# Pooled attention scores from 32-row tiles of TensorE instead of stacked operands

## The chip, the cores and the metric

The kernel runs on one core of one Trainium2 chip. The metric is the device time of one execution in microseconds. A core has TensorE (PE, matmuls, with its weight loads shown apart as PEld), VectorE (DVE), ScalarE (ACT), GpSimd (POOL), and SyncE (SP), which issues DMAs here.

## The reference

The input x is (4, 256, 32, 32): 4 images of 256 channels and 1024 pixels. Two residual blocks follow one another.

```python
x = x + L0(groupnorm(x))     # windowed attention (4 heads) beside pooled attention (4 heads)
x = x + L1(groupnorm(x))     # mask from the image's centre of mass, relu, 3x3 convolution
# pooled attention, per image: 1024 queries, 256 keys (means of 2x2 pixels), heads of 32
q = (xh.reshape(B, H*W, C) @ l_q_w).reshape(B, H*W, 4, 32)
k, v = (pooled @ l_kv_w) ...
attn = softmax(einsum('bnhd,bmhd->bhnm', q, k) * 32**-0.5)
lo = einsum('bhnm,bmhd->bnhd', attn, v)
# L1: mu = rounded centres of mass of x over rows and columns, per channel
mask = max(1 - (|posX - mu_x| + |posY - mu_y|) * mask_weight, -1)
out = conv3x3(relu(x * mask)) + bias
```

## The kernel before

The four images are taken one after the other. An image b passes `front(b)` (projections, pooled scores for their maxima, window scores) and `rest(b)` (softmax weights, sums, output projections, residual). The second block of image b-1 (statistics, mask, convolution) is laid between the steps of image b: its convolution is a list of 144 matmuls that TensorE works off in helpings, `conv.more(n)`, whose sizes stand in the tables FRONT and REST (lines 67 to 70). Image 0 has no convolution beside it, and neither has `front(1)`; there, `keep_warm` matmuls (table WARM) fill some gaps. Every engine has a written-out program, and semaphores order them against each other. What stands in an engine's program behind a wait stands still with it.

Precise products. Operands are split into a high part rounded to fp32r and a low remainder; a product is hi*hi + hi*lo + lo*hi, three matmuls for the projections. For the pooled scores the heads have 32 rows each, so the three products are made in one matmul of 96 rows: SyncE stacks the parts in SBUF, `qs` holding hi, lo, hi and `ks` hi, hi, lo of each head on rows 0 to 95 (`stack`, lines 240 to 254, six DMAs per image). `lq_hi`, `lq_lo`, `lk_hi`, `lk_lo` are made by ACT and DVE (lines 398, 400, 622, 627) from `slot[0]` and `slot[1]`. For this the columns of the pooled query and key weights are mixed on the host, so that the four heads of one dimension lie on neighbouring rows.

Largest scores. The softmax needs the maximum of each query over its 256 keys. TensorE computes the scores of 8 blocks of 128 queries (lines 969 to 992), 4 heads x 256 keys per block, into three PSUM slots of two banks each (LA_SLOT), and DVE reduces each block (`maxima`, line 633). The negated maxima are transposed (line 999), split in two (lines 641, 643), and SyncE lays them on rows 96 and 97 of `qs` (`stack_maxima`), against two rows of ones in `ks`. The scores proper, transposed (keys on partitions), are then 8 tiles of two matmuls of 98 rows and 512 columns (`pooled_scores`, line 904), each followed by an exponential on ACT (`exp_scores`, line 434). Tiles 0 and 1 stand in `front`, 2 and 3 and then 4 to 7 in `rest`. Their PSUM slots alternate (ST_SLOT). When all eight are exponentiated, `by_head` (line 912) sums them on column tiles of 32 columns.

Order around the change. On DVE, `front(b)` runs: the low parts; `masks(b-1)`, the statistics of the older image (17 to 20 small operations at its end, L505 to L517); `mask_parts(b-1)`, a chain of 16 small operations (L561 to L583); the maxima of blocks 0 to 5, 6 and 7; their split; `masked_image(b-1)` (L590), which waits for POOL's `mask_sum` (L297); the tiles of the convolution and the window softmax. POOL forms the products of queries and keys (L305), for which it waits until `mask_parts(b-1)` is through, and then the mask sums; in image 0 it prepares the convolution's weights around them (L313 to L341). ACT's program in `front(b)`: copies of the projections, the normalised older image (L415), `rectify` (L421) of its first half, then the copy of the window scores (L447), which TensorE transposes (L1008) for the window softmax.

TensorE's first block of largest scores waits for all six stacks (line 971), its later ones for the maxima of earlier blocks.

Of the kernel before, what the change touches and what calls it, by code (L numbers as in the profile page):

```python
# [5 lines left out]
F32 = mybir.dt.float32  # L6
# [6 lines left out]
P = 128  # L13
B, C, H, W = 4, 256, 32, 32
KT = C // P
# [10 lines left out]
SC = 3 * HD  # L26
SM = SC + 2
# [22 lines left out]
WCOLS = 6 * P  # L50


LA_SLOT = (0, 1, 2, 0, 1, 2, 0, 1)
ST_SLOT = (0, 1, 0, 1, 1, 0, 2, 1)
# [44 lines left out]
def build(nc, x, wqkv, whp, wlp, bh, bl, cw, cb, mw, filt, consts, selectors, out):  # L99
    with ExitStack() as ctx:  # L100
# [24 lines left out]
        qs = sb("qs", [P, HEADS, HW], F32R)  # L125
        ks = sb("ks", [P, HEADS, G], F32R)
# [10 lines left out]
        lq_hi, lq_lo = probs[:, 0].bitcast(F32R), probs[:, 1]  # L137
        lk_hi, lk_lo = probs[:, 2, 0:G].bitcast(F32R), probs[:, 2, G:2 * G]
# [50 lines left out]
        stacked, max_stacked = sem("stacked"), sem("max_stacked")  # L189
# [19 lines left out]
        def img(b, k, lo=0, n=HW):  # L209

            at = (b % RING) * KT * HW + k * HW + lo
            return xy[:, at:at + n]

# [7 lines left out]
        def _(sp):  # L221
# [18 lines left out]
            def stack(b):  # L240

                def rows(to, part, parts):
                    sp.dma_start(to[HD * part:HD * (part + 1)].bitcast(F32), parts.bitcast(F32)).then_inc(stacked, 16)  # L243

                sp.wait_ge(lq_act, b + 1)
                rows(qs, 0, lq_hi)
                rows(qs, 2, lq_hi)
                sp.wait_ge(lq_dve, b + 1)
                rows(qs, 1, lq_lo)
                sp.wait_ge(lk_act, b * 2 + 1)  # L250
                rows(ks, 0, lk_hi)
                rows(ks, 1, lk_hi)
                sp.wait_ge(lk_dve, b + 1)
                rows(ks, 2, lk_lo)

            def stack_maxima(b):

                sp.wait_ge(lm_dve, (b + 1) * 2)
                for i, t in enumerate((lm_hi, lm_lo)):
                    sp.dma_start(qs[SC + i:SC + i + 1].bitcast(F32), t.bitcast(F32)).then_inc(max_stacked, 16)  # L260

            def step(b, first, last):
# [3 lines left out]
                if not last:  # L266
                    stack(b + 1)
# [9 lines left out]
            stack(0)  # L277
# [9 lines left out]
        STACK, MAX_STACK = 6 * 16, 2 * 16  # L287
# [3 lines left out]
        def _(pool):  # L291
# [65 lines left out]
            nc.gpsimd.tensor_tensor(w_lo[:], raw_w, w_hi[:].bitcast(F32), ALU.subtract).then_inc(w_split, 1)  # L357
            pool.wait_ge(w_split, 2)
# [7 lines left out]
        def _(act):  # L366
# [28 lines left out]
            def projections(b, first):  # L395
                wait_count(act, lpv_pe, b)
                act.wait_ge(proj_pe, b * 5 + 1)
                nc.scalar.copy(lq_hi, flat[0]).then_inc(lq_act, 1)
                act.wait_ge(proj_pe, b * 5 + 2)
                nc.scalar.copy(lk_hi, slot[1][:, 0, 0:G]).then_inc(lk_act, 1)  # L400
# [743 lines left out]
```

## Time and profile before

| | |
|---|---|
| median of 3 runs | 425.68 us (424.81 to 427.03) |
| the profiled execution | 424.92 us, its span 423.1 us |
| TensorE matmuls busy | 336.3 us, 79% of the span, 1544 instructions |
| TensorE weight loads | 237.4 us, 56% |
| VectorE | 293.3 us, 69% |
| ScalarE | 114.1 us, 27% |
| GpSimd | 100.5 us, 24% |
| mean granted TensorE clock | 0.883 of full speed |

Times in rows are microseconds from the start of the span, means are ns. A matmul's duration contains its way through the array, so consecutive ones overlap: their pace is read from the starts, or from a merged row's length over its count. "<-" behind a group in brackets names what ended the idle time before it, and how long that was.

### The profile page before, as it was taken

The page shows a single profiled execution, that of the slowest core. Times are in us where ns is not written, and L with a number is a line of the kernel's source. Part 1 is how long each engine was busy: PE and PEld are TensorE (multiplying, and loading weights), DVE is VectorE, ACT ScalarE, POOL GpSimd, SP SyncE. Part 2 cuts the span into 40 slices and gives each one's busy share as a digit, 9 for nine tenths or more (in the row PEclk, how much of TensorE's full clock was granted, in tenths as well). Part 3 has the DMA queues.
Part 4 walks back from the last instruction along what each step waited for, and adds up shares of the span by engine and source line. Part 5 has one row for each costly group of instructions (what it writes and reads, how often), then busy time and mean ns, then how long its engine had stood idle before and what let it go on. Part 6 is the DMA issues. An engine that isn't in the chain of part 4 may idle for free.

```text
span 423.1 us, 4092 instructions
## 1 busy us (share of the span) xinstructions
PE 336.3 (79%) x1544; PEld 237.4 (56%) x1544; DVE 293.3 (69%) x584; ACT 114.1 (27%) x124; POOL 100.5 (24%) x58
## 2 busy tenths in 40 slices
PE   2580967899498599991999599965999999806996
PEld 1360725347374474681868373854877648705885
DVE  4940739877976987887679776896678658885121
ACT  2230014522402536133026243122046300231000
POOL 0288499200083020000910200006600200030000
PEclk9896895799859599997799989995999999965999
DMA  7579300006900000079000400293001001001011
GB/s 243 210 95 155 136 4 0 2 0 84 102 2 3 1 2 1 2 132 104 0 5 0 149 2 0 79 117 42 2 3 50 2 0 52 0 0 50 2 50 50
DMA packets 8611, 20.38 MB, mean 48 GB/s; under 512 B 1680, under 2 KB 4624, under 8 KB 8336
## 3 DMA queue, kind: packets, MB, share of 16 engines
q1 hardware_dynamic: 8592, 20.13, 23.8%
q8 instruction: 12, 0.20, 0.2%
q14 instruction: 7, 0.06, 0.1%
HBM read 7.93 MB, written 4.19 MB: 29 GB/s over the span
## 4 chain that ended last, share of the span: by engine, by line
PE 41%; issue 19%; DVE 16%; DMA 12%; POOL 5%; ACT 3%; SPq 2%; POOLq 0%; DVEq 0%; ACTq 0%
PE slot L838 18%; PE cps L870 17%; DMA ks<-probs 10%; PE cps L838 4%; POOL probs L305 4%; DMA xy<-x 2%; SPq L243 2%; DVE st L488 2%; ACT probs L434 1%; DVE gn L516 1%; POOL mask L297 1%; DVE v_lo L615 1%; PE slot L1008 1%; PE slot L1031 1%; DMA out<-xy 1%
## 5 line engine op out<-in xcount | busy, mean ns | idle before, releaser
L870 PE MATMUL cps<-v_hi,cw_hi 128*128 128x496 f32 (+1 forms) x192 | 79.1, 412 | 19.5 <-DVE xy L670 15.1
L870 PE MATMUL cps<-v_hi,cw_lo 128*128 128x496 f32 (+1 forms) x192 | 78.7, 410 | 0.0
L870 PE MATMUL cps<-v_lo,cw_hi 128*128 128x496 f32 (+1 forms) x192 | 77.8, 405 | 0.0
L305 POOL TENSOR_TENSOR probs<-q_w,k_w 128x1024 f32<-128x1024 f32 x16 | 37.3, 2363 | 139.2 <-DVE rw L583 132.2
L633 DVE TENSOR_REDUCE l_max<-slot 128x4 f32<-128x1024 f32 x32 | 37.7, 1220 | 33.5 <-PE slot L838 33.5
L870 PEld LDWEIGHTS cps<-v_hi,cw_hi 128*128 128x128 f32 x192 | 38.4, 200 | 32.9 <-ACT v_hi L428 20.6
L838 PE MATMUL slot<-ks,qs 96*128 96x256 f32 x128 | 26.5, 362 | 35.6 <-DMA ks<-probs 34.8
L838 PEld LDWEIGHTS slot<-ks,qs 96*128 96x128 f32 x128 | 23.8, 257 | 39.6 <-DMA ks<-probs 36.6
L870 PEld LDWEIGHTS cps<-v_hi,cw_lo 128*128 128x128 f32 x192 | 38.1, 198 | 8.4 <-issue 0.7
L870 PEld LDWEIGHTS cps<-v_lo,cw_hi 128*128 128x128 f32 x192 | 38.2, 199 | 7.1
L434 ACT ACTIVATE probs<-slot 128x1024 f32<-128x1024 f32 x32 | 31.7, 1024 | 36.1 <-PE slot L838 36.0
L838 PE MATMUL slot<-xn_hi,w_hi 128*128 128x512 f32 x60 | 25.1, 419 | 4.5 <-DVE xn_lo L526 4.5
L353 POOL TENSOR_TENSOR q_w<-q_w,k_w 128x1024 f32<-128x1024 f32 x4 | 9.6, 2391 | 75.8 <-DVE k_w L755 75.8
L421 ACT ACTIVATE xn<-mask 128x1024 f32<-128x1024 f32 x8 | 8.5, 1059 | 63.2 <-DVE mask L590 63.1
L838 PE MATMUL slot<-qs,ks 98*128 98x512 f32 x64 | 22.9, 468 | 2.0 <-DMA qs<-probs 1.7
L838 PE MATMUL slot<-xn_hi,w_lo 128*128 128x512 f32 x60 | 24.5, 408 | 0.0
L838 PE MATMUL slot<-xn_lo,w_hi 128*128 128x512 f32 x60 | 24.3, 405 | 0.0
L297 POOL TENSOR_TENSOR mask<-rw 128x1024 f32<-128x1024 f32 x8 | 15.2, 1916 | 38.2 <-DVE rw L583 38.2
L488 DVE BATCH_NORM_STATS2 st<-xy 128x6 f32<-128x512 f32 x32 | 19.8, 679 | 4.5 <-DMA xy<-x 4.5
L668 DVE SCALAR_TENSOR_TENSOR xy<-cps,cbias,xy 128x512 f32<-128x512 f32 x16 | 12.0, 748 | 14.8 <-PE cps L870 14.6
L838 PE MATMUL slot<-probs,cst 128*32 128x512 f32 x176 | 20.4, 596 | 1.9 <-ACT probs L434 1.9
L428 ACT CAST v_hi<-mask 128x1024 fp32r<-128x1024 f32 x16 | 16.7, 1046 | 14.2 <-DVE mask L608 7.2
(143 smaller groups left out, 545.4 us busy)
## 6 DMA issues: line engine op xcount, KB each, us to landing
qs<-probs SPq DMA_DIRECT2D x12, 512.0 KB, 10.6
xy<-x SPq DMA_DIRECT2D x8, 512.0 KB, 9.2
out<-xy SPq DMA_DIRECT2D x8, 512.0 KB, 2.6
raw_cw<-conv_w SPq DMA_DIRECT2D x2, 1152.0 KB, 7.5
ks<-probs SPq DMA_DIRECT2D x12, 128.0 KB, 13.6
probs<-h_qkv SPq DMA_DIRECT2D x2, 192.0 KB, 4.6
probs<-l_kv SPq DMA_DIRECT2D x2, 128.0 KB, 4.0
probs<-selectors SPq DMA_DIRECT2D x1, 256.0 KB, 4.0
```

What stands on the lines that cost most here:

```text
L243: sp.dma_start(to[HD * part:HD * (part + 1)].bitcast(F32), parts.bitcast(F32)).then_inc(stacked, 16)
L297: nc.gpsimd.tensor_tensor(mask[:, k].rearrange("p (h w) -> p h w", h=H), rw[:, k, 0].unsqueeze(2).to_broadcast([P, H, W]), rw[:, k, 1].uns ...
L305: nc.gpsimd.tensor_tensor(qk[:, j].rearrange("p (n w) -> p n w", n=NW), q_w[:].rearrange("p (n w) -> p n w", n=NW), k_w[:, j * G:(j + 1) * ...
L353: nc.gpsimd.tensor_tensor(pv[0], pv[0], pv[1], ALU.add).then_inc(pv_pool, 1)
L421: nc.scalar.activation(xn[:, k], mask[:, k], ACT.Relu).then_inc(relu, 1)
L428: nc.scalar.copy(v_hi[:, k, 2 * phase:2 * phase + 2].rearrange("p a b -> p (a b)"), mask[:, k]).then_inc(v_act, 1)
L434: nc.scalar.activation(probs[:, i], flat[ST_SLOT[i]], ACT.Exp, scale=SCALE / NW)\
L488: last = nc.vector.bn_stats(s[:, k, half], img(self.b, k, half * HALF, HALF))
L633: nc.vector.tensor_reduce(l_max[:, bass.ds(n, HEADS, step=NB)], flat[LA_SLOT[n]].rearrange("p (h m) -> p h m", h=HEADS), AX_X, ALU.max, ne ...
L668: ins = nc.vector.scalar_tensor_tensor(y, cps[:, pos], cbias[:, o:o + 1], y, ALU.add, ALU.add)
L838: return nc.tensor.matmul(dst, lhsT, rhs, start=start, stop=stop)
L870: ins = nc.tensor.matmul(cps[:, pos % 2, y0 * WT:y1 * WT], (cw_hi, cw_hi, cw_lo)[part][:, k, pos, dy + 1, o * P:(o + 1) * P], (v_hi, v_lo, ...
```

## The change

The stacks by DMA and the tiles `qs` and `ks` go. The columns of the pooled query and key weights are put in the order of the heads when they are split at the start (six parts each on ACT and POOL in place of one), so that head h lies on rows 32h to 32h+31 of `lq_hi`, `lq_lo`, `lk_hi`, `lk_lo`, which get tiles of their own. Each product of the split is a matmul of its own on the 32 rows of its head, and the products accumulate in PSUM, in a bank per head: step by step, the four heads of a step behind one another. The maxima go to rows 32h and 32h+1 of a tile `top`, against a tile of ones, as a fourth step of two rows. Largest scores are made for two blocks at a time (24 matmuls of 256 columns), and the scores proper in four parts (16 matmuls of 512 columns), each followed by two exponentials. On DVE, the mask chain `mask_parts(b-1)` moves behind the maxima and their split. POOL's products wait for the statistics of the older image instead of its mask chain.

```diff
-            def stack(b):
-                def rows(to, part, parts):
-                    sp.dma_start(to[HD * part:HD * (part + 1)].bitcast(F32), parts.bitcast(F32)).then_inc(stacked, 16)
...
             def stack_maxima(b):
...
-                    sp.dma_start(qs[SC + i:SC + i + 1].bitcast(F32), t.bitcast(F32)).then_inc(max_stacked, 16)
+                    sp.dma_start(top[i:P:HD].bitcast(F32), t.bitcast(F32)).then_inc(max_stacked, 16)
...
-            stack(0)
             load(1)
             load(2)
...
-                wait_count(pool, mask_c, b * N_MASK)
+                wait_count(pool, gn_c[1], b * N_GN)
                 products(b)
...
-            nc.gpsimd.tensor_tensor(w_lo[:], raw_w, w_hi[:].bitcast(F32), ALU.subtract).then_inc(w_split, 1)
+            for (lo, hi), source in zip(weight_parts(w_lo, w_hi), weight_sources()):
+                nc.gpsimd.tensor_tensor(lo, source, hi.bitcast(F32), ALU.subtract).then_inc(w_split, 1)
...
+                    part, pair = divmod(i, 2)
+                    t, half = divmod(part, 2)
                     act.wait_ge(st_pe, b * LT + i + 1)
-                    nc.scalar.activation(probs[:, i], flat[ST_SLOT[i]], ACT.Exp, scale=SCALE / NW)
+                    nc.scalar.activation(probs[:, pair * 2 * MT + t:pair * 2 * MT + t + MT + 1:MT,
+                                               half * HALF:(half + 1) * HALF],
+                                         slot[ST_SLOT[part][pair]][:], ACT.Exp, scale=SCALE / NW)
...
                 if not first:
                     masks(b - 1)
-                    mask_parts(b - 1)
                 maxima(b, range(6))
                 older_result(V_SUM)
                 maxima(b, range(6, NB))
                 maxima_parts(b)
+                if not first:
+                    mask_parts(b - 1)
                 older_result(V_DIFF)
...
+            def pooled_scores(b, part):
+                t, half = divmod(part, 2)
+                m, q = slice(t * P, (t + 1) * P), halves(half)
+                for step in range(4):
+                    for h in range(HEADS):
+                        r = rows_of(h)
+                        to = slot[ST_SLOT[part][h // 2]][:, h % 2]
+                        if step < 3:
+                            ins = mm(to, (lk_hi, lk_hi, lk_lo)[step][r, m], (lq_hi, lq_lo, lq_hi)[step][r, q],
+                                     step == 0, False)
+                        else:
+                            r = slice(HD * h, HD * h + 2)
+                            ins = mm(to, one[r], top[r, q], False, True)
+                            if h % 2:
+                                ins.then_inc(st_pe, 1)
+
+            def largest_scores(b, n):
+                for block in range(2):
+                    q = slice((n + block) * P, (n + block + 1) * P)
+                    for step in range(3):
+                        for h in range(HEADS):
+                            r = rows_of(h)
+                            ins = mm(slot[LA_SLOT[n + h // 2]][:, h % 2, block * G:(block + 1) * G],
+                                     (lq_hi, lq_lo, lq_hi)[step][r, q], (lk_hi, lk_hi, lk_lo)[step][r],
+                                     step == 0, step == 2)
+                            if step == 2 and block == 1 and h % 2:
+                                ins.then_inc(la_pe, 1)
...
-                for n in range(NB):
+                for n in range(0, NB, 2):
                     if n == 0:
-                        pe.wait_ge(stacked, (b + 1) * STACK)
-                        pe.wait_ge(qkv_sb, b * 3 + 2)
...
+                    else:
+                        pe.wait_ge(la_max, b * NB + n - 1)
+                        if n == 2 and not first:
                             pe.wait_ge(gn_c[1], (b - 1) * N_GN + GN_SENT + 1)
...
+                    largest_scores(b, n)
...
                     conv.more(FRONT[2 + n])
+                    conv.more(FRONT[3 + n])
                     if starting:
                         keep_warm(WARM[1 + n])
...
-                for i in range(2, LT - NW):
-                    pe.wait_ge(st_exp, b * LT + i - 1)
-                    pooled_scores(b, i)
-                    conv.more(REST[1])
+                pe.wait_ge(st_exp, b * LT + 2)
+                pooled_scores(b, 1)
+                conv.more(2 * REST[1])
...
-                for i in range(LT - NW, LT):
-                    if i < LT - 1:
-                        pe.wait_ge(pv_ready, b * NW + i - 2)
-                    else:
-                        pe.wait_ge(st_exp, b * LT + 5)
-                    pooled_scores(b, i)
-                    conv.more(REST[4])
+                for part in range(2, NW):
+                    pe.wait_ge(pv_ready, b * NW + part + 1)
+                    pe.wait_ge(st_exp, b * LT + part + 2)
+                    pooled_scores(b, part)
+                    conv.more(2 * REST[4])
```

The helper `weight_parts` yields the query, key and value columns, the pooled value columns, and for each of the two channel tiles the pooled query and the pooled key columns; `weight_sources` yields the same from the raw weights, with the mixed columns put in order. `maxima` reads the two heads and two blocks of a slot and writes them to their places in `l_max`.

## Rows read from the trace of the kernel before

**Rows 1.** Waits: engine, line, releaser: us in total, times, longest.
```profile
PE slot L838 <- DMA ks<-probs: 34.8, 4, 10.9
```
**Rows 2.** DMA issues: count, KB of each, median us from issue to landing.
```profile
ks<-probs SPq DMA_DIRECT2D x12, 128.0 KB, 13.6
```
**Rows 3.** Busy time by stretch: the stalls of images 0, 2 and 3, and after.
```profile
core 0: us, PE busy (x) PEld busy (x) DVE busy (x) ACT busy (x) POOL busy (x), PEclk, DMA share, GB/s
30.50:41.40 10.90, 0.01 (x1) 0.00 (x0) 0.00 (x0) 1.01 (x1) 9.88 (x7) 0.70 1.06 130
...
192.40:201.30 8.90, 0.00 (x0) 0.00 (x0) 6.43 (x35) 3.38 (x3) 1.20 (x1) 0.66 0.89 98
...
281.90:290.80 8.90, 0.18 (x1) 0.00 (x0) 6.63 (x35) 3.38 (x3) 0.99 (x1) 0.62 0.90 99
290.80:296.90 6.10, 6.07 (x20) 5.37 (x21) 3.49 (x3) 0.00 (x0) 6.10 (x4) 0.50 0.00 1
```
**Rows 4.** Timeline of PE and its loads: start, length, engine, operation, count.
```profile
47.38 1.60 PE L838 MATMUL slot<-ks,qs 96*128 96x256 f32 x12
...
163.08 3.64 PE L838 MATMUL slot<-probs,cst 128*32 128x512 f32 x32 [0.21 <-ACT probs L434]
165.25 0.13 PEld L838 LDWEIGHTS slot<-probs,cst 128*32 128x32 f32 x4 [0.30 <-issue]
166.65 1.98 PE L838 MATMUL slot<-q_w,w_out 128*128 128x512 f32 x4
...
183.03 0.30 PEld L838 LDWEIGHTS slot<-w_hi,p_w 128*128 128x128 f32 x2
```
**Rows 5.** Timeline of the start and of image 0's front.
```profile
10.13 3.45 POOL L357 TENSOR_TENSOR w_lo<-probs,w_hi 128x1536 fp32r<-128x1536 f32 x1 [9.19 <-ACT w_hi L440]
10.32 3.27 DVE L516 SCALAR_TENSOR_TENSOR gn<-gn 128x2 f32<-128x2 f32 x1
...
30.55 1.01 ACT L407 COPY k_w<-slot 128x1024 f32<-128x1024 f32 x1 [1.79 <-PE slot L838]
...
37.07 3.56 POOL L326 TENSOR_TENSOR cw_lo<-raw_cw,cw_hi 128x768 fp32r<-128x768 f32 x2
...
47.62 9.30 POOL L305 TENSOR_TENSOR probs<-q_w,k_w 128x1024 f32<-128x1024 f32 x4 [6.99 <-PE cps L838]
```
**Rows 6.** Timeline of the rest of image 0.
```profile
64.03 1.94 ACT L434 ACTIVATE probs<-slot 128x1024 f32<-128x1024 f32 x2 [1.97 <-PE slot L838]
...
67.77 1.97 PE L1031 MATMUL slot<-cst,k_w 128*128 128x128 f32 x8 [0.53 <-DVE k_w L657]
...
74.78 2.36 DVE L755 TENSOR_TENSOR xn<-slot,v_w 128x1024 f32<-128x1024 f32 x2 [0.18 <-PE slot L838]
...
80.58 2.78 PE L838 MATMUL slot<-probs,cst 128*32 128x512 f32 x24 [1.30 <-ACT probs L434]
```
**Rows 7.** Timelines of DVE, ACT and PE in image 3's front.
```profile
285.75 0.16 DVE L517 SCALAR_TENSOR_TENSOR gn<-gn 128x2 f32<-128x2 f32 x1
...
304.37 1.23 DVE L633 TENSOR_REDUCE l_max<-slot 128x4 f32<-128x1024 f32 x1 [0.23 <-PE slot L838]
...
309.60 1.00 ACT L447 COPY q_w<-slot 128x1024 f32<-128x1024 f32 x1
...
311.52 1.04 PE L1008 MATMUL slot<-cst,q_w 128*128 128x128 f32 x8
```
**Rows 8.** Timeline of DVE in the tail: mask chain's end, first masked image.
```profile
369.57 0.19 DVE L583 TENSOR_SCALAR rw<-rw 128x64 f32<-128x64 f32 x1
...
371.79 2.91 DVE L590 SCALAR_TENSOR_TENSOR mask<-mask,xn 128x1024 f32<-128x1024 f32 x1 [2.02 <-POOL mask L297]
```
**Rows 9.** Timeline of DVE: end of statistics and start of softmax, image 2.
```profile
196.05 0.16 DVE L517 SCALAR_TENSOR_TENSOR gn<-gn 128x2 f32<-128x2 f32 x1
...
221.90 0.29 DVE L650 TENSOR_REDUCE s_max<-slot 128x32 f32<-128x128 f32 x1 [1.57 <-PE slot L1008]
```
**Rows 10.** Timelines of DVE and PE: last maxima and transposes of image 1.
```profile
129.16 2.36 DVE L633 TENSOR_REDUCE l_max<-slot 128x4 f32<-128x1024 f32 x2 [4.56 <-PE slot L838]
...
135.72 1.09 PE L1008 MATMUL slot<-cst,q_w 128*128 128x128 f32 x8 [1.94 <-ACT q_w L447]
```

More of the change, by code:

```diff
@@ L25 @@
 LT = HEADS * MT
-SC = 3 * HD
-SM = SC + 2
 NB = HW // P
@@ L124, in build @@
         v_w = sb("v_w", [P, HW])
-        qs = sb("qs", [P, HEADS, HW], F32R)
-        ks = sb("ks", [P, HEADS, G], F32R)
+        lq_hi, lq_lo = sb("lq_hi", [P, HW], F32R), sb("lq_lo", [P, HW], F32R)
+        lk_hi, lk_lo = sb("lk_hi", [P, G], F32R), sb("lk_lo", [P, G], F32R)
+        top = sb("top", [P, HW], F32R)
+        one = sb("one", [P, P], F32R)
         lv = sb("lv", [P, MT, P])
@@ L212, in img, with weight_parts, weight_sources @@
             return xy[:, at:at + n]
+        def weight_parts(*tiles):
+            yield [t[:, :, 0:WLQ] for t in tiles]
+            yield [t[:, :, WLV:WCOLS] for t in tiles]
+            for k in range(KT):
+                for c0 in (WLQ, WLK):
+                    yield [t[:, k, c0:c0 + P].rearrange("p (h d) -> p h d", h=HEADS) for t in tiles]
+        def weight_sources():
+            yield raw_w[:, :, 0:WLQ]
+            yield raw_w[:, :, WLV:WCOLS]
+            for k in range(KT):
+                for c0 in (WLQ, WLK):
+                    yield raw_w[:, k, c0:c0 + P].rearrange("p (d h) -> p h d", h=HEADS)
         def run(step):
@@ L439, in step @@
                     act.wait_ge(w_in, 3 * KT * 16)
-                    nc.scalar.copy(w_hi[:], raw_w).then_inc(w_split, 1)
+                    for (hi,), source in zip(weight_parts(w_hi), weight_sources()):
+                        last_part = nc.scalar.copy(hi, source)
+                    last_part.then_inc(w_split, 1)
                     normalise_first()
@@ L810, in _ @@
             nc.vector.tensor_copy(sel[:].rearrange("p a b -> p (a b)"), raw_sel).then_inc(w_ready, 1)
-            nc.vector.memset(ks[SC:SM].bitcast(F32), 1.0).then_inc(ones, 1)
+            nc.vector.memset(one[:].bitcast(F32), 1.0).then_inc(ones, 1)
             nc.vector.scalar_tensor_tensor(mwf[:, 2], mwf[:, 1], 1.0, mwf[:, 0], ALU.is_equal,
@@ L902, in project, with rows_of @@
                 last.then_inc(proj_pe, 1)
-            def pooled_scores(b, i):
-                h, t = divmod(i, MT)
-                for half in range(2):
-                    last = mm(slot[ST_SLOT[i]][:, half], ks[0:SM, h, t * P:(t + 1) * P], qs[0:SM, h, halves(half)],
-                              True, True)
-                last.then_inc(st_pe, 1)
+            def rows_of(h):
+                return slice(HD * h, HD * (h + 1))
+            def pooled_scores(b, part):
[24 more added lines that the diff above has]
+                                ins.then_inc(la_pe, 1)
             def by_head(s, lhsT, ready):
@@ L978, in front @@
                             pe.wait_ge(qkv_sb, b * 3 + 3)
-                    elif n == 2:
-                        if not first:
+                    else:
+                        pe.wait_ge(la_max, b * NB + n - 1)
+                        if n == 2 and not first:
                             pe.wait_ge(gn_c[1], (b - 1) * N_GN + GN_SENT + 1)
-                    else:
-                        pe.wait_ge(la_max, b * NB + n - 2)
-                    for h in range(HEADS):
-                        ins = mm(flat[LA_SLOT[n]][:, h * G:(h + 1) * G], qs[0:SC, h, n * P:(n + 1) * P], ks[0:SC, h],
-                                 True, True)
-                    ins.then_inc(la_pe, 1)
+                    largest_scores(b, n)
                     if first and n == 2:
@@ L1014, in front @@
                 pe.wait_ge(max_stacked, (b + 1) * MAX_STACK)
-                for i in range(2):
-                    pooled_scores(b, i)
+                pooled_scores(b, 0)
                 conv.more(FRONT[12])
```

48 lines of the change are left out of this document (18 added, 30 removed).

## The prediction

> **What bounds the kernel now.** I read the waits first: TensorE (PE) loses 34.8 us in four waits for the stacked key rows, the largest item it has [rows 1]. The stack DMAs take 13.6 us (median) from issue to landing [rows 2]. Taken alone that promises 35 us. So I read, for each wait, what the other engines did in it, in the busy times by stretch [rows 3]. In image 0 VectorE (DVE) stands still (0.00 of 10.9 us), but GpSimd (POOL) is busy 9.88 us with the convolution weights. In images 2 and 3 (image 1 repeats it) DVE is busy 6.43 and 6.63 of 8.9 us: it does the statistics and the mask chain of the older image, behind which the maxima queue. The granted clock is 0.62 to 0.70 over these stretches, that is, it falls from 2.4 to 1.2 GHz in each, and 0.50 in the 6.1 us of dense work after the last one. Most of the stall is therefore covered, and the question is what comes last once it is gone.
>
> **How fast row tiles run.** No row tile of 32 rows stands in this trace. The nearest rows are the column tiles of by_head: 32 instructions of 512 columns take 3.64 us while the same type at full width takes 1.98 us for 4 [rows 4]. That is 0.43 us for one full-width instruction and 0.43 us for four column tiles: four run at once, and four loads sit in 0.13 us. Full-width fp32r at 256 columns goes at 1.60/12 = 0.13 us, 0.117 us without the tail of the last; I double this at half clock [rows 4]. A pair of blocks is now 24 matmuls in place of 8. Four at once: 6 x 0.117 = 0.7 us, plus 0.2 to 0.3 us for two changes between tile shapes (3.64 us for eight groups of 0.43 leaves 0.2) = 1.0 us against 0.94 before. One at a time: 24 x 0.117 = 2.8 us. I take four at once. A scores part is 16 matmuls of 512 columns for what were 4: 0.93 us four at once (3.7 us one at a time), so only the shape changes are added.
> TensorEngine Tiling (Array Packing), in the Trainium skill, says under "Key Properties" that tiles work independently but that a change of tiling mode drains TensorE; under "PSUM Pressure" it says different row tiles may not share a bank, which the change respects. TensorE: Matmul & The Clock Gate (Trainium skill), Part 3, states 3.07x measured for four row tiles of 512 columns; by it a part would take 3.7/3.07 = 1.2 us, an estimate 0.3 us over mine, or 1.2 us an image.
>
> **Start: -0.9 us (0 to -1.8).** One w_lo subtraction of 3.45 us becomes six. From the subtractions of 768 and 1536 columns (about 1.8 and 3.45 us [rows 5]) POOL's fixed part is 0.2 us, so six take 4.5 us; ScalarE's (ACT) six casts take about 2.2 us for 1.47. w_lo ends at 15.3 us, before PE needs it (17.4). But now a DVE operation of normally 0.16 us stands for 3.27 us, exactly to the end of POOL's [rows 5]: they exclude each other. Shorter and later pieces let the chain through earlier by 0.8 to 1.6 us. The loads of images 1 and 2, which SP now issues after the convolution weights with no stack in front, queue behind these weights; I cost them at nothing.
>
> **Image 0, front: -7.0 us (-4.4 to -7.5).** k_w is copied by 31.56 [rows 5], so the pairs start there, not at 41.46. The V projection then ends by 37. What is last now is POOL: its convolution weights end at 40.63, and only then do the products start (47.62 now). The gain is 7.0, not 10. The products and the window scores follow at the old pace. If the clock falls in the 2.3 us before the first product, the last scores and the transposes cost 2.6 more.
>
> **Image 0, rest: +3.7 us (+2.7 to +4.7).** Each part fills both slots and releases its two exponentials at its end; the next part waits for them. Before, tiles alternated between the slots. Part 0 ends at 64.85 as now, its exps run 64.9 to 66.8 (now 64.0 to 66.0), part 1 runs 66.9 to 68.9 and pushes the transposes from 67.77: +1.2 [rows 6]. Part 2 needs the third product (76.0, now 77.2): 1.9 us at half clock, one exp 1.0, part 3 1.9, two exps 2.0, joints 0.3: by_head at 84.3 where it was 80.58.
>
> **Images 1 to 3, front.** The maxima can begin when the statistics end, S, ahead of the 16 operations of the mask chain, 3.7 us earlier than now. Image 3: S is 285.9 [rows 7]; the first pair runs at 283.1 to 284.0 (v_w copied); maximum 0 ends at 287.1; pair 1.0, 13 convolution matmuls 3.0, pair 1.0, 10 of them 2.3, pair 1.0, two maxima 2.4: the maxima end at 297.8 where they ended at 305.6 [rows 7]. 7.8 us gained there. Now the bill. The transpose and the two splits take 1.2 us, the moved mask chain 3.8 us (16 small operations, none hidden). Then POOL's mask sum, which ran beside the maxima, is exposed. The tail of the kernel shows this very sequence: from the end of the chain at 369.77 to the end of the first masked image at 374.70 are 4.9 us, because the DVE operation (2.91 us in place of 1.21) also stands until POOL's second sum ends [rows 8]. SBUF — State Buffer, "Who interferes with whom", in the Trainium skill, states this: a VectorE instruction with two SBUF inputs and a GpSimd one that reads SBUF exclude each other; the trace agrees. Behind it ACT's queue holds rectify (as long) and then the copy of the window scores (1.00) [rows 7], for which PE waits. 297.8 + 1.2 + 3.8 + 4.9 + 2.0 = 309.7: the transposes come 1.8 us earlier than at 311.52, and PE has idled 5.9 us for it. By the stalls seen, its clock falls there: transposes 0.9 us longer (1.97 against 1.04 [rows 6, 7]), 1.5 us on what follows: +0.6. With weight 0.6 it has also fallen in the 3.1 us between the first pair and the second, which costs 2.0 more: **image 3 +1.9 us (-1.7 to +3.8)**.
> Image 2 likewise: S at 196.2, the maxima end at 208.1, the transposes start at 220.1 against 221.0 (0.9 ahead of the softmax's first operation) [rows 9], clock +1.0, and 0.6 x 2.0, less where DVE and not PE is last: **+0.8 (-1.9 to +2.5)**. In image 1 there is no convolution yet to fill PE, and the warming matmuls between blocks 5 and 7 fall away: at half clock a pair takes 1.6 us, the maxima end at 124.8 (131.5 now), the transposes start at 136.8 (135.7 now) [rows 10] and take 0.9 longer: **+1.9 (-0.6 to +2.8)**.
>
> **Images 1 to 3, rest: +1.5 us (0 to +3.6).** Four parts with 0.2 us of shape changes each, and one more exp behind the last part, under 8 convolution matmuls (1.8 us): 0.5 an image. The third product is there when part 2 wants it.
>
> **Sum:** -0.9 - 7.0 + 3.7 + 1.9 + 0.8 + 1.9 + 1.5 = +1.9. On the profiled execution's 424.9 that gives 426.8 us, no change that can be told from none (about 0.5%, 2.1 us, is what a measurement of this kernel can tell). The median shown, 425.7, lies 0.8 above the profiled execution, which the range takes in.
>
> **Rivals.**
> (a) Row tiles take turns: slower. Its place is the 96 + 64 matmuls per image, its point the pace: slower as soon as a pair takes clearly over 1.2 us. If only the loads (two of 128 columns in 0.30 us, of which one lasts 0.19: one per 0.11 us [rows 4]) take turns, a pair is 2.7 and a part 1.8 us: about 2 us on each of three pairs and 0.9 on each part, at half clock double: +10, +9, +8, +9 us on top, 463. If matmuls too: 2.8 and 3.7 us, some 485. For it: no row tile is in the trace. Against: column tiles plainly run four at once. Chance 0.12.
> (b) PE keeps its clock in the shorter gaps: faster. Image 0's rest is then +2.7, images 1 to 3 -0.6, -0.9, -1.2 and the rest 1.2: -7 us, 418. For it: the gaps of 3 us are half the old ones. Against: 5.9 us of new idling per image. Chance 0.20.
> (c) The stall was the bound and most of 34.8 us comes off: 390 to 400. DVE's and POOL's busy shares in it [rows 3] speak against. Chance 0.04.
> The forecast has 0.62, with its own range 421 to 432; 0.02 is left for what I don't see.
>
> **Chances and range.** Faster by over 0.5% is under 423.5: (b), (c) and a sixth of the forecast's own, 0.33. Slower by over 0.5% is over 427.8: (a) and 0.4 of the forecast's own, 0.39. The same: 0.28. The range reaches over (b), 415 to 434, and leaves out (a) and (c).
>
> **What would show it.** The pace of the 32-row matmuls (0.7 us for 24 of 256 columns); POOL's first products at 40 us; by_head of image 0 later relative to the products by 3.7; in images 1 to 3 maxima that end 7 us earlier and then a PE wait of 4 to 6 us for ACT's copy of the window scores; the masked image at 2.9 us instead of 1.2. The forecast is wrong if row tiles are slower than 0.12 us per group of four, if the clock stays up, or if DVE is not held by POOL's sum.

## The result and the profile after

| | kernel before | changed kernel |
|---|---|---|
| median of its runs, us | 425.6 (424.8 to 427.0) | 434.95 (433.8 to 436.4) |
| ratio to before | 1 | 1.022, 95% interval 1.017 to 1.027 |
| profiled execution, us | 424.9 | 433.85 |
| its span, us | 423.1 | 432.1 |
| mean granted clock | 0.883 | 0.869 |

The change costs 2.2%. The forecast was 426.8 with a range that ends at 434.0, so it had the direction and a fifth of the size.

The waits of the changed kernel (engine, line, what released it: us in total, times, longest) no longer have the 34.8 us of [rows 1]. New ones stand in their place:

```profile
POOL mask L294 <- DVE rw L586: 64.9, 4, 39.1
...
PE slot L1035 <- ACT q_w L450: 19.9, 4, 7.7
...
PE slot L845 <- DVE l_max L637: 14.1, 7, 2.9
...
DVE mask L593 <- POOL mask L294: 6.8, 4, 2.0
```

19.9 us of TensorE's new idle time stand ahead of the transposes of the window scores. The timeline of image 2 (start, length, engine, line, operation) shows the sequence behind that wait on VectorE, GpSimd, ScalarE and TensorE:

```profile
210.83 0.28 DVE L647 CAST probs<-slot 32x128 fp32r<-32x128 f32 x1 [0.42 <-PE slot L1026]
...
214.95 0.20 DVE L586 TENSOR_SCALAR rw<-rw 128x64 f32<-128x64 f32 x1
...
215.23 3.78 POOL L294 TENSOR_TENSOR mask<-rw 128x1024 f32<-128x1024 f32 x2 [9.91 <-DVE rw L586]
...
217.18 4.05 DVE L593 SCALAR_TENSOR_TENSOR mask<-mask,xn 128x1024 f32<-128x1024 f32 x2 [1.37 <-POOL mask L294]
...
220.12 1.06 ACT L419 ACTIVATE xn<-mask 128x1024 f32<-128x1024 f32 x1 [21.95 <-DVE mask L593]
221.09 0.99 ACT L450 COPY q_w<-slot 128x1024 f32<-128x1024 f32 x1
...
222.14 1.97 PE L1035 MATMUL slot<-cst,q_w 128*128 128x128 f32 x8 [5.64 <-ACT q_w L450]
```

The maxima end at 210.4 (214.9 before), and then every step is exposed: 3.8 us of mask chain, GpSimd's sum, the masked image (4.05 us for two, of which the first takes 2.91 as in [rows 8]), rectify, copy. TensorE, which was busy up to its transposes before, stands idle for 5.64 us. Its clock falls: from the transposes at 222.14 it runs at 1.2 GHz for 7.9 us, to 230.0. A second slow stretch stands further back, from 247.7 to 254.0, behind a wait for the statistics of the next image. The busy times by stretch give the size of both together: from the transposes to by_head of image 2, before and after (columns as in [rows 3]):

```profile
220.80:252.80 32.00, 26.65 (x121) 21.22 (x119) 25.25 (x56) 13.16 (x15) 2.35 (x1) 0.95 0.14 50
```
```profile
222.10:259.70 37.60, 33.15 (x168) 24.30 (x170) 26.31 (x57) 14.00 (x16) 2.35 (x1) 0.80 0.11 42
```

32.0 us became 37.6, TensorE's busy time grew by 6.5 us, and its granted clock went from 0.95 to 0.80.

Where the 9.0 us of span came from, read from the start times of the same steps in both timelines (S is the end of the statistics of the older image, as in the prediction; us):

| stage | before | after | difference | forecast |
|---|---|---|---|---|
| start and image 0 up to its transposes | 59.98 | 52.19 | -7.8 | -7.9 |
| image 0, on to by_head | 20.60 | 23.44 | +2.8 | +3.7 |
| by_head of image 0 to S of image 1 | 33.51 | 35.64 | +2.1 | 0 |
| image 1, S to transposes, to by_head | 21.63, 27.36 | 23.04, 28.32 | +2.4 | +2.4 |
| image 2, S to transposes, to by_head | 24.61, 31.94 | 26.37, 37.52 | +7.3 | +1.3 |
| image 3, S to transposes, to by_head | 25.61, 25.00 | 25.70, 28.12 | +3.2 | +2.4 |
| by_head of images 1 and 2 to the next S | 33.14 | 33.14 | 0.0 | 0 |
| by_head of image 3 to the end | 86.6 | 85.5 | -1.1 | 0 |

The sum is +9.0 where +1.9 was forecast, and 6.0 of the 7.1 us of miss are in image 2. The lines of image 0's by_head and of the end scatter by more than a microsecond between kernels whose code there is the same (below), so little is built on them. The row tiles themselves ran as forecast. One part of the pooled scores in image 2 is four groups of four, 0.23 us apart:

```profile
236.03 0.51 PE L845 MATMUL slot<-lq_hi,lk_hi 32*128 32x512 f32 x4
236.37 0.41 PE L845 MATMUL slot<-lq_lo,lk_hi 32*128 32x512 f32 x4
236.60 0.41 PE L845 MATMUL slot<-lq_hi,lk_lo 32*128 32x512 f32 x4
236.83 0.41 PE L845 MATMUL slot<-top,one 2*128 2x512 f32 x4
237.17 0.49 PE L877 MATMUL cps<-v_hi,cw_hi 128*128 128x496 f32 x1
```

From 236.03 to 237.17 are 1.14 us, and a pair of blocks takes 0.91 us, read in the same way (299.99 to 300.90). In image 0 GpSimd's products start at 39.89 in place of 47.62 [rows 5], right behind its convolution weights, and the w_lo pieces hold VectorE for 1.66 us in place of 3.27:

```profile
11.30 1.66 DVE L520 SCALAR_TENSOR_TENSOR gn<-gn 128x2 f32<-128x2 f32 x1
...
36.29 3.63 POOL L323 TENSOR_TENSOR cw_lo<-raw_cw,cw_hi 128x768 fp32r<-128x768 f32 x2
39.89 9.24 POOL L302 TENSOR_TENSOR probs<-q_w,k_w 128x1024 f32<-128x1024 f32 x4
```

### The profile page after: what moved, and what is told of

Same layout as the page of the kernel before. It is cut to its first block, busy times and chain, and to the rows that moved or that the text cites. A ratio compares the mean times of both kernels' runs of the same rounds, so it can differ in the third digit from the quotient of the medians.

```text
span 432.1 us, 4949 instructions
## 1 busy us (share of the span) xinstructions
PE 343.4 (79%) x1976; PEld 230.4 (53%) x1976; DVE 298.1 (69%) x584; ACT 114.3 (26%) x129; POOL 103.1 (24%) x63
## 4 chain that ended last, share of the span: by engine, by line
PE 45%; DVE 21%; issue 19%; POOL 9%; ACT 3%; DMA 1%; POOLq 0%; SPq 0%; DVEq 0%; ACTq 0%
PE cps L877 22%; PE slot L845 20%; DVE st L491 2%; POOL probs L302 2%; DVE l_max L637 2%; POOL mask L294 2%; POOL cw_lo L323 2%; PE cps L845 2%; DVE mask L593 2%; ACT probs L434 1%; DVE xn L552 1%; DMA xy<-x 1%; PE slot L1035 1%; DVE q_w L762 1%; DVE xn L549 1%
## 5 line engine op out<-in xcount | busy, mean ns | idle before, releaser
L877 PE MATMUL cps<-v_hi,cw_hi 128*128 128x496 f32 (+1 forms) x192 | 80.1, 417 | 18.8 <-DVE xy L676 15.1
L877 PE MATMUL cps<-v_hi,cw_lo 128*128 128x496 f32 (+1 forms) x192 | 79.6, 415 | 0.0
L877 PE MATMUL cps<-v_lo,cw_hi 128*128 128x496 f32 (+1 forms) x192 | 78.9, 411 | 0.0
L877 PEld LDWEIGHTS cps<-v_hi,cw_hi 128*128 128x128 f32 x192 | 38.6, 201 | 33.5 <-ACT v_hi L426 19.8
L637 DVE TENSOR_REDUCE l_max<-slot 128x4 f32<-128x1024 f32 x32 | 37.6, 1219 | 18.6 <-PE slot L845 18.6
L845 PE MATMUL slot<-xn_hi,w_hi 128*128 128x512 f32 x60 | 25.2, 421 | 3.8 <-POOL w_lo L355 3.8
L845 PE MATMUL slot<-lk_hi,lq_hi 32*128 32x256 f32 x128 | 12.5, 380 | 18.5 <-DVE l_max L637 14.1
L845 PE MATMUL slot<-probs,cst 128*32 128x512 f32 x176 | 24.2, 692 | 2.1 <-ACT probs L434 2.0
L1035 PE MATMUL slot<-cst,q_w 128*128 128x128 f32 x32 | 7.0, 391 | 19.9 <-ACT q_w L450 19.9
L674 DVE SCALAR_TENSOR_TENSOR xy<-cps,cbias,xy 128x512 f32<-128x512 f32 x16 | 11.9, 747 | 13.4 <-PE cps L877 13.4
L593 DVE SCALAR_TENSOR_TENSOR mask<-mask,xn 128x1024 f32<-128x1024 f32 x8 | 16.2, 2061 | 6.8 <-POOL mask L294 6.8
L676 DVE SCALAR_TENSOR_TENSOR xy<-cps,xy 128x512 f32<-128x512 f32 x16 | 10.7, 687 | 14.4 <-PE cps L877 14.4
```

The costliest lines, as they stand in the source:

```text
L593: nc.vector.scalar_tensor_tensor(mask[:, k], mask[:, k], -1.0, xn[:, k], ALU.max, ALU.mult).then_inc(masked, 1)
L637: nc.vector.tensor_reduce(l_max[:, 0:HEADS * NB].rearrange("p (h n) -> p h n", n=NB) [:, 2 * pair:2 * pair + 2, block:block + 2], slot[LA_ ...
L674: ins = nc.vector.scalar_tensor_tensor(y, cps[:, pos], cbias[:, o:o + 1], y, ALU.add, ALU.add)
L676: ins = nc.vector.scalar_tensor_tensor(y, cps[:, pos - 2], (1.0, -1.0)[pos - 2], y, ALU.mult, ALU.add)
L845: return nc.tensor.matmul(dst, lhsT, rhs, start=start, stop=stop)
L877: ins = nc.tensor.matmul(cps[:, pos % 2, y0 * WT:y1 * WT], (cw_hi, cw_hi, cw_lo)[part][:, k, pos, dy + 1, o * P:(o + 1) * P], (v_hi, v_lo, ...
```

## The experiments

Theory A: the loss comes from the second half of the change, the mask chain behind the maxima. It puts chain, GpSimd's sum, masked image and rectify ahead of ScalarE's copy, and TensorE's idle time and the clock behind it are the price. Theory B: the row tiles cost it (changes of shape, both exponentials of a part at its end). All ratios are to the kernel before, run on the same chip in the same session; its median there was 425.6 to 427.1 us, so medians of different sessions compare to a microsecond or two.

| kernel | median us | ratio, 95% interval |
|---|---|---|
| changed kernel | 434.95 | 1.022, 1.017 to 1.027 |
| e1_chain_ahead | 422.8 | 0.992, 0.989 to 0.995 |
| e2_chain_behind | 450.9 | 1.057, 1.052 to 1.063 |
| e3_copy_first | 427.5 | 1.002, 0.998 to 1.005 |
| e4_warm | 436.9 | 1.025, 1.020 to 1.031 |
| e5_warm_fit | 428.0 | 1.008, 1.004 to 1.012 |
| e6_refill | 414.4 | 0.976, 0.969 to 0.982 |
| e7_ahead_copy | 422.7 | 0.992, 0.988 to 0.996 |
| e8_pool_free | 447.9 | 1.053, 1.046 to 1.059 |
| e9_refill_copy | 410.6 | 0.964, 0.959 to 0.969 |
| e10_before_refill | 422.6 | 0.992, 0.988 to 0.995 |
| e11_refill_warm0 | 414.1 | 0.973, 0.967 to 0.979 |
| e12_all | 410.35 | 0.964, 0.959 to 0.969 |

The same stages as above, in the profiled executions (us; for each of images 1, 2, 3: S to transposes, then transposes to by_head):

| kernel | S to transposes | transposes to by_head |
|---|---|---|
| before | 21.6, 24.6, 25.6 | 27.4, 31.9, 25.0 |
| changed | 23.0, 26.4, 25.7 | 28.3, 37.5, 28.1 |
| e1 | 20.2, 24.2, 23.1 | 28.3, 33.9, 26.3 |
| e2 | 27.8, 30.6, 30.5 | 28.5, 35.3, 26.1 |
| e3 | 16.4, 19.4, 20.8 | 33.9, 39.9, 33.5 |
| e4 | 25.0, 28.5, 28.5 | 28.4, 33.7, 26.2 |
| e5 | 23.0, 26.6, 26.5 | 27.9, 32.6, 26.4 |
| e6 | 20.1, 20.2, 20.9 | 28.1, 33.7, 25.9 |
| e9 | 16.5, 19.3, 19.3 | 31.0, 33.0, 26.0 |
| e10 | 20.4, 23.5, 22.0 | 27.2, 31.8, 25.0 |

### The two halves of the change, one by one

e1_chain_ahead is the changed kernel with the mask chain back in its old place:

```diff
-                wait_count(pool, gn_c[1], b * N_GN)
+                wait_count(pool, mask_c, b * N_MASK)
...
                 if not first:
                     masks(b - 1)
+                    mask_parts(b - 1)
                 maxima(b, range(6))
...
                 maxima_parts(b)
-                if not first:
-                    mask_parts(b - 1)
```

> The changed kernel with one part undone: the mask chain stands ahead of the maxima again and GpSimd's products wait for it again; row tiles, accumulation in PSUM and the missing stack DMAs stay. Theory A (the loss of the change lies in TensorE's idle time ahead of the window-score transposes, 19.9 us in four waits, 5.6 us each in images 2 and 3, and in the half clock behind it): GpSimd's mask sum hides beside the maxima again, the masked image takes 1.2 us in place of 2.9, ScalarE's copy comes some 3.5 us earlier in each of three images, and the clock stays up behind the transposes of image 2, worth 3 more: about 421 us, 418 to 425. Theory B (the row tiles themselves cost it, by changes of shape and by parts whose exponentials both come at the end): the time stays at 433 to 436.

e2_chain_behind makes the opposite edit in the kernel before: mask_parts behind maxima_parts, GpSimd's wait on gn_c[1]; the stacks stay.

> The kernel before with only the other part of the change: the mask chain behind the maxima, GpSimd's products let go by the statistics; stacks by DMA and full-width score matmuls stay. Theory A: before, the chain (3.8 us) ran inside the wait for the stacks, so moving it gives back nothing and exposes chain, GpSimd's sum, the slow masked image and rectify: 6 to 8 us in each of three images, 443 to 450 us. Theory B: the placement is worth little either way, 424 to 429 us.

Measured: 422.8 us, inside theory A's 418 to 425, and 450.9 us, just above its 443 to 450. Theory B falls as the account of the loss. Row tiles alone make the kernel 0.8% faster; the placement alone makes it 5.7% slower. But row tiles are not free: by the table e1 gains 4.4 us from S to the transposes of images 1 to 3 and gives 4.3 us back from the transposes to by_head (1.0, 2.0 and 1.3 us), so that its 0.8% comes from image 0. How much of the 4.3 us is the clock and how much the scores themselves is not taken apart here. In e1 GpSimd's sum (206.65 to 210.4) is done before the masked image asks for it, and the two masked images take 2.35 us and not 4.05 (timeline of VectorE, image 2):

```profile
212.80 0.76 DVE L674 SCALAR_TENSOR_TENSOR xy<-cps,cbias,xy 128x512 f32<-128x512 f32 x1
213.47 2.35 DVE L593 SCALAR_TENSOR_TENSOR mask<-mask,xn 128x1024 f32<-128x1024 f32 x2
```

In e2 the waits show both idle times of TensorE side by side, because the stacks still set the start of the maxima and moving the chain away gives nothing back:

```profile
PE slot L839 <- DMA ks<-probs: 35.1, 4, 11.1
PE slot L1009 <- ACT q_w L447: 21.6, 4, 9.5
```

By the table e2 loses 5 to 6 us from S to the transposes in each image, and up to 3.4 behind them. Beside row tiles the placement costs 12 us (434.95 against 422.8), not 24, since the maxima there do begin 3.7 us earlier. That gain stands in the prediction's sum; it is smaller than the bill. That the 12 us between 24 and 12 are this gain (3 x 3.7 = 11 us) is worked out, not measured by itself.

### The wait or the clock behind it

e3_copy_first takes the wait away by order alone:

```diff
                 if not first:
                     normalise_y(b - 1, b + 1)
-                    rectify(b - 1, 0)
                 act.wait_ge(ssum_pe, b + 1)
                 nc.scalar.copy(q_w[:], flat_cps if first else flat[0]).then_inc(ssum_sb, 1)
                 if not first:
+                    rectify(b - 1, 0)
                     rectify(b - 1, 1)
```

> The changed kernel, but ScalarE copies the window scores before it rectifies the first half of the masked image, so that the mask chain is no longer ahead of TensorE's transposes. Theory A: TensorE's wait for this copy goes from 19.9 us to under 4, the transposes come 6 us earlier, the clock stays up behind them; VectorE's softmax still stands behind the masked image, so of the 6 us only 1.5 and the clock's share (some 4 in image 2, 1 to 2 in images 1 and 3) come off: 425 to 429 us. Theory B: 433 to 436 us.

Measured: 427.5 us, inside theory A's 425 to 429. The wait did not vanish, it moved (waits of TensorE in e3): TensorE now comes early to the convolution of the new image and waits there for VectorE.

```profile
PE cps L877 <- DVE v_lo L618: 17.3, 3, 8.7
...
PE slot L1035 <- ACT q_w L449: 2.0, 2, 1.2
```

e4_warm and e5_warm_fit leave the order alone and put matmuls without a use into the wait (14 in e4; in e5 9 in image 1 and 7 in images 2 and 3, as shown):

```diff
                 conv.more(FRONT[11])
+                if not first:
+                    for _ in range(9 if starting else 7):
+                        mm(slot[1][:, 0, 0:C_ALL], cst[:, C_ID:C_ID + P], cst[:, 0:C_ALL], True, True)
                 pe.wait_ge(ssum_sb, b + 1)
```

> The changed kernel with 14 matmuls of 384 columns without a use (about 0.34 us each at 2.4 GHz, 4.8 us) into a free bank, ahead of the wait for ScalarE's copy of the window scores in images 1 to 3. The wait itself stays, only the clock behind it can change. If the half clock behind the wait is the larger part of the price: by_head of image 2 comes 4 us earlier, of image 3 and 1 about 2 us each, 427 to 430 us. If the wait itself is the price and the clock hardly matters: 434 to 436 us.

> As e4_warm, but the matmuls without a use are sized to end inside the wait: in e4_warm one took 0.66 us and not 0.34, so that the 14 took 9.2 us and pushed the transposes by 2 to 3 us an image, while from the transposes to by_head images 2 and 3 took 3.9 and 1.9 us less. Now 7 in images 2 and 3 (4.6 us in a wait of 5.6) and 9 in image 1. If the half clock is the price: the transposes come no later than in the changed kernel, by_head follows them 3.9 and 1.9 us sooner, 0.9 comes off the transposes of image 1: 427.5 to 430 us. If the shorter stage of e4_warm was only a catching up of what was lost before it: 434 to 436 us.

e4 gave 436.9 us, which taken alone would speak against the clock. Its trace says otherwise. I had the price of such a matmul wrong: it is two instructions and 0.66 us, so the 14 took about 9 us and pushed the transposes by 2.0, 2.1 and 2.8 us in images 1 to 3. In e5 they fit (timeline of TensorE, image 2):

```profile
216.91 4.68 PE L845 MATMUL slot<-cst 128*128 128x384 f32 x14
222.69 1.09 PE L1038 MATMUL slot<-cst,q_w 128*128 128x128 f32 x8 [1.11 <-ACT q_w L450]
```

The transposes come as late as ever (26.6 us behind S, 26.4 in the changed kernel), but they take 1.09 us and not 1.97, and the stretch behind them is (columns as in [rows 3])

```profile
222.70:255.30 32.60, 28.17 (x164) 20.85 (x164) 25.91 (x57) 13.91 (x16) 2.35 (x1) 0.95 0.13 49
```

32.6 us at a clock of 0.95 instead of 37.6 at 0.80. The same stretch is 0.45 us shorter in image 1 and 1.7 us in image 3, 7.1 us in all; 1.1 us are lost ahead of the transposes of images 2 and 3, so 6.0 are left, and the medians differ by 7.0 (434.95 and 428.0). The two profiled executions differ by only 4.0 us (433.85 and 429.87): 0.8 us in image 0 and 1.1 us behind by_head of image 3, where both kernels issue the same code, go the other way. e4 repeats the reading: from the transposes to by_head its images 2 and 3 take 3.9 and 1.9 us less than in the changed kernel. A kernel that does the changed kernel's work, with ScalarE's copy no earlier, gets back 6 to 7 of the 9 us when TensorE is kept busy until it comes. So of the loss against the kernel before the larger part is the clock behind the wait, not the wait. e1, which has neither in images 2 and 3, is 5 us faster than e5.

### VectorE beside GpSimd's products

e8_pool_free is e1 without the second edit: GpSimd's products are let go by the statistics and run beside the mask chain.

```diff
-                wait_count(pool, mask_c, b * N_MASK)
+                wait_count(pool, gn_c[1], b * N_GN)
```

> e1_chain_ahead, but GpSimd's products are let go by the statistics, as in the changed kernel, and so run beside the 16 operations of the mask chain. If VectorE's operations with two inputs and GpSimd's products exclude each other (in the changed kernel the masked image took 2.91 us in place of 1.21 beside GpSimd's sum), the first of them stands for up to 2.4 us, and those behind it for a product each where GpSimd is let in again: the chain takes 6 to 10 us in place of 3.7 and the time goes to 430 us or more. If they share, the chain stays at 3.7 us, the products end 3.7 us earlier and nothing waits for that: 421 to 424 us.

Measured: 447.9 us, 25 more than e1. The timelines of GpSimd and VectorE in image 1:

```profile
112.48 9.23 POOL L302 TENSOR_TENSOR probs<-q_w,k_w 128x1024 f32<-128x1024 f32 x4 [42.20 <-DVE gn L520]
...
112.55 0.29 DVE L566 TENSOR_REDUCE mu<-rw 128x4 f32<-128x128 f32 x1
112.87 1.98 DVE L568 TENSOR_TENSOR gn<-mv,gn 128x2 f32<-128x2 f32 x1
114.88 2.26 DVE L569 SCALAR_TENSOR_TENSOR gn<-gn 128x2 f32<-128x2 f32 x1
117.17 2.27 DVE L570 TENSOR_SCALAR gn<-gn 128x2 f32<-128x2 f32 x1
119.48 0.17 DVE L571 RECIPROCAL gn<-gn 128x2 f32<-128x2 f32 x1
119.68 2.05 DVE L572 TENSOR_TENSOR gn<-gn 128x2 f32<-128x2 f32 x1
```

Each of the four products holds one operation of 0.16 us until it ends: 3.8 us of chain become 11.7, in all three images alike, which makes 24 us for the 25 measured. The reduction and the reciprocal pass. This is why the place of the chain and GpSimd's wait belong together: the changed kernel could let the products go at S only because the chain had left. SBUF — State Buffer, "Who interferes with whom", in the Trainium skill, names the same split: operations with two SBUF inputs, and tensor_scalar where its operands let it take both ports, can be held by GpSimd, tensor_reduce on this chip never; the trace agrees (2.27 us for L570, 0.29 for L566).

### A version that beats both

e1 still idles 25.2 us in seven waits for maxima, 6.7 us in each of images 1 to 3 between the first and the second pair. e6_refill puts convolution matmuls there (the new entries of WARM act in image 1 alone):

```diff
-FRONT = (0, 0, 0, 0, 8, 5, 5, 5, 5, 5, 6, 10, 23)
+FRONT = (0, 0, 20, 0, 5, 3, 4, 3, 3, 3, 4, 9, 18)
-WARM = (5, 0, 0, 0, 0, 0, 6, 1, 2, 4, 4)
+WARM = (5, 9, 0, 2, 0, 2, 0, 2, 2, 4, 4)
```

> e1_chain_ahead, in which TensorE waits 6.7 us between the first and the second pair of blocks in each of images 1 to 3 (for the maxima behind the mask chain) and then runs the second pair at half clock. Here 20 of the 72 convolution matmuls of the front are moved into that wait (4.5 us), the later helpings are smaller, and in image 1 some matmuls without a use stand there and between the pairs. If TensorE's queue sets the end of the maxima once the chain has stopped: they end 3 us earlier in images 2 and 3 and 1.5 in image 1, 414 to 418 us. If VectorE sets it: no more than 1 us an image, 419.5 to 422 us.

> e1_chain_ahead with ScalarE's copy of the window scores ahead of rectify. In e1_chain_ahead the transposes of images 2 and 3 find TensorE busy up to them, and the softmax starts as they end (307.70 to 308.73, softmax 308.77). If the copy is on the path the transposes and the softmax come up to 1.1 us earlier in each of three images: 419.5 to 421.5 us. If TensorE's own queue sets them: 422 to 424 us, as e1_chain_ahead.

> e6_refill with ScalarE's copy of the window scores ahead of rectify. In e6_refill the maxima of image 1 end as GpSimd's mask sum starts, and TensorE waits 4.7 us for that copy; in images 2 and 3 only 1 us. If the copy is on the path: image 1's transposes come 3 to 4 us earlier, but VectorE's softmax still stands behind the masked image, so 1 us there and up to 1 in each other: 412 to 414 us. If VectorE's order alone sets the softmax: 414 to 415 us, as e6_refill.

> The kernel before, with the same 20 convolution matmuls moved into its own wait for the stacks (8.9 us in images 2 and 3), nothing else changed. If the wait was worth filling whatever the form of the scores: the work moved (4.5 us) comes off behind it and the clock does not fall so low, 3 us in each of images 2 and 3: 418 to 421 us, and the row tiles are worth the 4 us that e6_refill (414.4) is below it. If the convolution helpings between the maxima were hidden beside VectorE anyway: 424 to 427 us.

e6: 414.4 us. The wait for maxima is (e1, then e6)

```profile
PE slot L844 <- DVE l_max L637: 25.2, 7, 6.7
```
```profile
PE slot L844 <- DVE l_max L637: 7.2, 5, 1.9
```

and TensorE's queue did set the end of the maxima: they end 14.1 and 15.7 us behind S in images 2 and 3, 18.3 and 17.2 in e1. The copy ahead of rectify is worth nothing in e1 (e7, 422.7: TensorE is busy up to its transposes), but 3.8 us once the wait is filled (e9, 410.6, below the 412 to 414 expected), because then ScalarE's queue is the last to come. The same edit changes its worth with what stands next to it.

e10 is the control: the same 20 matmuls moved into the wait for the stacks of the kernel before, with FRONT = (0, 20, 0, 0, 5, 3, ...). It gives 422.6 us, 3 less than before and not the 5 to 8 expected. TensorE's wait for the stacks remains:

```profile
PE slot L838 <- DMA ks<-probs: 26.6, 4, 11.7
```

So with 20 matmuls moved into the wait in both forms the row tiles are worth 8 us (422.6 against 414.4 of e6 and 414.1 of e11). e6 has matmuls without a use in image 1 besides, which e10 has not; image 1 takes 48.2 us from S to by_head in e6, 48.5 in e1, which is without them, and 47.5 in e10, so they don't make the difference. 6.3 of them are gained by the middle of image 0 (by_head at 75.60 in place of 81.91), where no convolution exists to fill anything.

e11_refill_warm0 and e12_all put `keep_warm(3)` ahead of by_head in image 0; e12 also has e9's copy.

> e6_refill with 3 matmuls without a use (0.66 us each) in image 0's 2.0 us wait for the last two exponentials. In the changed kernel by_head of image 0 takes 5.77 us at half clock behind this wait, in the kernel before 3.64 us behind one of 1.3 us. If the wait is what lets the clock fall: by_head takes 3.7 us and 2 us come off, 412 to 413 us. If the clock is low there for another reason: 414 to 415 us.

> All of it in one kernel: row tiles, mask chain ahead of the maxima, refilled wait, copy ahead of rectify, matmuls without a use ahead of by_head in image 0. The sum of the shares expected of the other kernels of this set: 410.5 to 413 us; if neither of the two small edits is worth anything, 414 to 415 us.

e11: 414.1 us, no gain. The three matmuls ran at half clock and took 4.21 us in a wait of 2.0, so by_head began 2.9 us later (78.46 for 75.60) and took 3.77 us in place of 6.36: an even trade. e12: 410.35 us, as e9 (there the three took 3.54 us and by_head 3.64). Either is 3.6% below the kernel before and 5.7% below the changed kernel.

Image 0 gave one more reading, against my own account. By_head takes 3.64 us in the kernel before and 5.77 in the changed one, and I took the longer wait ahead of it (2.02 for 1.30 us) for the reason. But e2 and e10 issue in image 0 exactly what the kernel before issues, with the same wait, and show (kernel before, then e2)

```profile
80.58 3.64 PE L838 MATMUL slot<-probs,cst 128*32 128x512 f32 x32 [1.30 <-ACT probs L434]
```
```profile
81.00 6.39 PE L839 MATMUL slot<-probs,cst 128*32 128x512 f32 x32 [1.30 <-ACT probs L434]
```

In e10 the same 32 matmuls take 6.48 us. So the clock of this stretch differs from execution to execution of one and the same code, and the +2.1 us of the table is not shown to be the change's.

## Why the prediction failed

By its own steps:

- **What bounds the kernel.** Right: nearly none of the 34.8 us came off in images 1 to 3, and image 0 gained what the products allowed. Rival (c) had no part in it.
- **Speed of row tiles.** Right to a tenth: pair 0.91 us for 1.0, part 1.14 us for 1.13. Rival (a) is out. The prediction set the ratio of 3.07 for four row tiles, from TensorE: Matmul & The Clock Gate, Part 3, in the Trainium skill, beside its own: by it a part would take 1.2 us, an estimate. The trace does not bear it out in this stream: four tiles every 0.23 us, the pace of one full-width matmul of 512 columns, speak for 4.
- **Start and image 0's front.** Right in the sum, -7.8 for -7.9, with some luck in its parts: the first projection came 0.3 us earlier and not 0.9 (17.10 for 17.39), the front gained 7.5 and not 7.0.
- **Image 0's rest.** +2.8 for +3.7, right in kind. The slow by_head behind it (+2.1 us) was not in the sum; by e2 and e10 it can come in the kernel before as well.
- **Images 1 to 3, front: the mechanism.** Right in every link: chain 3.8 us, sum and masked image 4.9 us (215.15 to 220.09), rectify and copy 2.0 us, TensorE idle 5.6 us for 5.9. The clock drop before the second pair happened each time, where the sum took 0.6 of its 2.0 us: in images 2 and 3 the maxima end 14.7 and 14.0 us behind S in place of the 11.9 that both were given without a drop, 2.8 and 2.1 us (second pairs at 196.96 and 293.99). Mostly by this image 2 was under-sized by 2.0 us ahead of its transposes: +1.8 us measured (26.37 for 24.61), where its +0.8 holds -0.2 when the clock term of 1.0 is taken out.
- **The failed step: the price of the clock behind the new idle time, "clock +1.0" in image 2 above all.** The mechanism was right and the term was mis-sized. The sum has 0.9 us for image 1, 1.0 for image 2 and 2.4 for image 3 ("transposes 0.9 us longer, 1.5 us on what follows", of which +0.6 is left after the 1.8 us gained), 4.3 in all. The runs give 0.45, 4.9 and 1.7 us, 7.1 in all (e5 against the changed kernel); in image 2 e4 gives 3.9. So image 2 was short by 3.9 us (2.9 by e4), and image 3 was priced too high. In image 2 the drop reaches through the transposes (+0.9), the part (+0.9) and nine convolution matmuls (3.97 us for 2.07 in e5), and the products of VectorE, which wait for TensorE here, come 3.6 us later. Then TensorE waits 4.38 us for the statistics, in e5 too. Behind that wait half clock lasts 6.3 us (247.7 to 254.0) in the changed kernel and 3.2 us (244.6 to 247.8) in e5, 1.3 us more. This last part is not shown to be the first drop's: e4, which kept its clock as e5 did, has the same wait of 4.38 us and 5.9 us of half clock behind it (249.4 to 255.3). The sum had one short drop, with VectorE as cover in image 2, where TensorE was the last to come. With the 2.0 us ahead of the transposes and 0.2 in the rest the 3.9 us make, up to rounding, image 2's 6.0. The three waits and the first matmul back at 2.4 GHz behind each (timelines of TensorE, changed kernel, e5, e4):

```profile
247.70 0.59 PE L845 MATMUL slot<-mv,cst 128*128 128x4 f32 x2 [4.38 <-DVE mv L498]
...
254.08 0.40 PE L845 MATMUL slot<-top,one 2*128 2x512 f32 x4
```
```profile
244.63 0.59 PE L845 MATMUL slot<-mv,cst 128*128 128x4 f32 x2 [4.38 <-DVE mv L498]
...
248.14 0.39 PE L877 MATMUL cps<-v_hi,cw_lo 128*128 128x496 f32 x1
```
```profile
249.38 0.59 PE L845 MATMUL slot<-mv,cst 128*128 128x4 f32 x2 [4.38 <-DVE mv L498]
...
255.33 0.39 PE L845 MATMUL slot<-lq_hi,lk_lo 32*128 32x512 f32 x4
```

- **Images 1 to 3, rest.** With the clock kept (e5) it is 0.5, 0.7 and 1.4 us for 0.5 each: 1.1 us under-sized in total.
- **Rivals and range.** Rival (b), TensorE keeps its clock, would have been 418; e5 keeps it behind the transposes only, not before the second pair, and takes 428.0. The own range of the forecast ended at 432, and the range on record at 434.0, 1 us below the time. The bound that did not hold is image 2's: +2.5, with at most 1.2 us of rest, for a measured +7.3. The clock behind the wait stood in it with one value.
- **What the prediction could not see.** It costed both halves of the change as one and never asked what row tiles would give without the move. The answer lay in its own numbers: with the chain in its old place 3.7 of the 7.8 us are not gained in the maxima, but chain, sum and slow masked image (3.8 + 4.9 us) shrink to one masked image of 1.2, some 4 us an image in favour of e1; 12 us were measured.

## What to carry to other kernels

When an edit opens a new idle stretch on TensorE, price the slow clock by what is queued behind it and who waits for that, with a range, and not by the wait alone; here keeping the clock gave back 6 to 7 of 9 us. Split a change into its halves before costing it: the half that looked like the enabler (the chain behind the maxima) cost 12 us and the other gave 3 to 8. And fill the wait that a removed transfer leaves with work that is already on that engine's list; that turned 422.8 into 414.4 us, and only then did a swap of two ScalarE operations bring another 3.8.

## What the runs showed of the hardware

- Four row tiles of 32 rows in four PSUM banks run at the pace of one full-width matmul: 0.117 us for a group of four with 256 columns, 0.23 with 512, also for tiles of which only 2 rows are used. The two changes of shape around such a block cost 0.2 us together.
- A matmul of fp32 data with 384 columns is two instructions; one took 0.66 us at 2.4 GHz and 1.4 at 1.2 GHz.
- A small VectorE operation (0.16 us) beside GpSimd's products waits for one product, 2.0 to 2.3 us, and the next operation meets the next product; tensor_scalar with one input is held too (2.27 us), reduction and reciprocal are not (0.29 and 0.17 us; e8).
- The clock behind a wait of 1.3 us is not fixed by the code: by_head of image 0 took 3.64 us in one execution and 6.39 and 6.48 us in two others of the same instructions.
- The length of the slow stretch behind a wait is not fixed by the wait either: behind the same 4.38 us of idle time in image 2 TensorE stayed at 1.2 GHz for 6.3 us in the changed kernel, 5.9 us in e4 and 3.2 us in e5. It does not follow from an earlier drop alone, for e4 and e5 had both kept their clock behind the wait before.
